# A macaron block's attention stage: normalisation of the next batch in four steps, earlier statistics, and two token tiles

## The reference, cut to what matters

```python
x = x + 0.5 * _L0_ffn_ref(_layernorm(x), ...)
x = x + _L0_attn_ref(_layernorm(x), wq, w_down, wk_up, wv_up, wo)
x = x + 0.5 * _L0_ffn_ref(_layernorm(x), ...)

def _L0_attn_ref(x, wq, w_down, wk_up, wv_up, wo):   # 16 heads of 16
    q = rope(x @ wq); lat = x @ w_down
    k = rope(lat @ wk_up); v = lat @ wv_up
    scores = einsum('bqhd,bkhd->bhqk', q, k) * scale     # 512 x 512 per head
    scores = where(page of key <= page of query, scores, min)
    return einsum('bhqk,bkhd->bqhd', softmax(scores), v) @ wo
```

## Time and profile before

| what | value |
| --- | --- |
| median of 3 runs | 1954.05 us |
| the profiled execution | 1956.1 us, span of its trace 1954.0 us |
| mean granted TensorE clock | 0.974 of full |
| PE / DVE / ACT / POOL busy | 92% / 68% / 56% / 43% |
| first and last step of attention with `x` | load issued 564.6 us, last load issued 1241.3 us |

### The profile page before, as it was taken

One profiled execution on the slowest core, in us unless ns is written; L12 is line 12 of the kernel. 1 busy time (PEld: TensorE's weight loads), 2 busy tenths in 40 slices (PEclk: granted clock), 3 DMA queues, 4 the chain that ended last, 5 costly groups with the idle time before them and its releaser, 6 DMA issues. The chain is left out here.

```text
span 1954.0 us, 31890 instructions
## 1 busy us (share of the span) xinstructions
PE 1788.5 (92%) x10553; PEld 1098.4 (56%) x10554; DVE 1337.6 (68%) x3338; ACT 1095.2 (56%) x2260; POOL 836.5 (43%) x923
## 2 busy tenths in 40 slices
PE   6999998999955789999999999999799999989998
PEld 3666665777732344444455454445455656567776
DVE  4878787566537567777777777778268787866664
ACT  4767675111114567777777777776566767631111
POOL 1111110677646565555555555551000101027777
PEclk9999999999978899999999999999999999999999
DMA  2324341899943233333333333332213243339997
GB/s 81 120 86 135 96 125 63 247 258 252 246 74 86 78 85 104 99 95 105 100 98 99 104 102 95 107 91 68 66 49 106 93 139 93 106 97 265 262 265 157
DMA packets 192653, 244.05 MB, mean 125 GB/s; under 512 B 17578, under 2 KB 159978, under 8 KB 192494
## 3 DMA queue, kind: packets, MB, share of 16 engines
q1 hardware_dynamic: 166654, 202.97, 34.6%
q0 software_dynamic: 24576, 37.77, 10.1%
q10 hardware_dynamic: 1264, 1.31, 0.2%
HBM read 126.63 MB, written 63.86 MB: 97 GB/s over the span
## 5 line engine op out<-in xcount | busy, mean ns | idle before, releaser
L1352 DVE TENSOR_REDUCE a_smax<-a_p_ring 128x1 f32<-128x512 f32 (+2 forms) x768 | 353.7, 505 | 151.7 <-PE a_p_ring L1439 146.9
L1257 ACT ACTIVATE a_probs<-a_p_ring 128x512 f32<-128x512 f32 x640 | 364.1, 607 | 103.3 <-PE a_p_ring L1451 102.1
L1439 PE MATMUL a_p_ring<-p_ks,p_qs 100*128 100x512 bf16 (+3 forms) x1024 | 244.9, 304 | 43.2 <-ACT a_probs L1257 20.0
L48 POOL TENSOR_TENSOR f_rstd<-f_mv,eps 128x4 f32<-128x4 f32 x32 | 26.2, 818 | 539.0 <-DVE f_mv L42 534.5
L1451 PE MATMUL a_p_ring<-p_qs,p_ks 103*128 103x512 bf16 (+3 forms) x1024 | 243.7, 305 | 6.0 <-ACT a_probs L1257 5.3
L648 ACT ACTIVATE e_silu<-e_p_up 128x176 f32<-128x176 f32 x128 | 40.6, 317 | 352.8 <-PE e_p_up L738 352.8
L487 PE MATMUL f_p_up<-f_xnT,ws1T 128*128 128x512 f32 x384 | 186.8, 609 | 1.1 <-ACT f_xnT L280 1.1
L528 PE MATMUL f_p_z<-ws2T,f_hidden 128*128 128x256 f32 (+1 forms) x768 | 183.9, 390 | 1.9 <-DVE f_hidden L374 1.9
L127 POOL DMA_INDIRECT h_got<-rows,slot_token x128 | 126.0, 984 | 135.1 <-DVE slot_token L464 86.1
L1467 PE MATMUL a_p_out<-a_probs,p_v 128*32 128x512 f32 (+3 forms) x2048 | 176.6, 445 | 6.5 <-ACT a_probs L1257 6.5
L487 PE MATMUL f_p_up<-f_xnT,ws3T 128*128 128x512 f32 x384 | 180.6, 593 | 0.0
(11 more groups left out here) (156 smaller groups left out, 3573.7 us busy)
## 6 DMA issues: line engine op xcount, KB each, us to landing
h_w<-w_in SPq DMA_DIRECT2D x128, 352.0 KB
p_qs<-a_parts SPq DMA_DIRECT2D x192, 128.0 KB, 2.4
p_ks<-a_parts SPq DMA_DIRECT2D x192, 128.0 KB, 2.5
h_w<-w_in SPq DMA_DIRECT2D x128, 176.0 KB
rows<-f_row SPq DMA_DIRECT2D x32, 640.0 KB, 6.4
x<-x_in SPq DMA_DIRECT2D x16, 512.0 KB, 5.9
acc<-x SPq DMA_DIRECT2D x16, 512.0 KB, 3.3
a_x<-acc SPq DMA_DIRECT2D x16, 512.0 KB, 4.0
```

Source lines behind the costliest of these rows:

```text
L1257: nc.scalar.activation(to[:], p_score[s][:], ACT.Exp, scale=SCALE).then_inc(score_free[s], 1)
L1352: ins = nc.vector.tensor_reduce(smax[:, t, 4 * g + h:4 * g + h + 1], p_score[s][:, at:at + length], AX.X, ALU.max)
L1439: ins = nc.tensor.matmul(p_score[s][:, at:at + length], qs[1 - u][0:SR + MASK, 4 * g + h, t * P:(t + 1) * P], ks[1 - u][0:SR + MASK, 4 * g ...
```

## The change

`x` becomes two tiles, batch n in `x[n % 2]`, with a load semaphore each. Batches 0 and 1 are both loaded at the start, ahead of the residual; after `XT 1` of batch j SP now loads j + 2 where it loaded j + 1. `NORM` becomes four steps of one activation each. In the turns, `STATS` move from 0.57 to 0.785 down to 0.30 to 0.43, and the one `NORM` at 0.87 becomes four at 0.595 to 0.715. In the opening lists, the statistics and normalisation of batch 1 come right after the transposes of batch 0; `V` of batch 0 and `XT` and `LAT` of batch 1 come before the first scores instead of among them; the statistics and normalisation of batch 2 move from the last tenth of `FIRST_SCORES` to 0.12 to 0.32.

```diff
-NEXT_INPUT = [(0.57, ("STATS", 0)), (0.61, ("STATS", 1)), (0.65, ("STATS", 2)), (0.785, ("STATS", 3)),
-              (0.87, ("NORM",))]
+NEXT_INPUT = [(0.30, ("STATS", 0)), (0.34, ("STATS", 1)), (0.38, ("STATS", 2)), (0.43, ("STATS", 3)),
+              (0.595, ("NORM", 0)), (0.635, ("NORM", 1)), (0.665, ("NORM", 2)), (0.715, ("NORM", 3))]
...
-FIRST_INPUT = of_batch(-2, [("XT", 0), ("XT", 1), ("Q", 0), ("LAT", 0), ("SWAP", 0), ("K", 0), ("SWAP", 1),
-                            ("Q", 1), ("K", 1), ("SWAP", 2), ("HIGH", 0), ("HIGH", 1), ("SPLIT", 0), ("SPLIT", 1),
-                            ("STACK", 0), ("SWAP", 3), ("STATS", 0), ("STATS", 1), ("STATS", 2), ("STATS", 3),
-                            ("NORM",)])
+FIRST_INPUT = (of_batch(-2, [("XT", 0), ("XT", 1), ("STATS", 0), ("STATS", 1), ("STATS", 2), ("STATS", 3),
+                             ("NORM", 0), ("NORM", 1), ("NORM", 2), ("NORM", 3),
+                             ("Q", 0), ("LAT", 0), ("SWAP", 0), ("K", 0), ("SWAP", 1), ("Q", 1), ("K", 1), ("SWAP", 2),
+                             ("HIGH", 0), ("HIGH", 1), ("SPLIT", 0), ("SPLIT", 1), ("STACK", 0)])
+               + of_batch(-1, [("V", 0), ("V", 1), ("XT", 0), ("XT", 1)]) + of_batch(-2, [("SWAP", 3)])
+               + of_batch(-1, [("LAT", 0)]))
 FIRST_SCORES = steps_of(
...
-    + at_places(-1, [(0.01, ("V", 0)), (0.03, ("V", 1)), (0.05, ("XT", 0)), (0.08, ("XT", 1)), (0.11, ("LAT", 0)),
-                     (0.15, ("Q", 0)), (0.365, ("NEG", 0)), (0.37, ("SWAP", 0)), (0.20, ("K", 0)), (0.38, ("SWAP", 1)),
+    + at_places(-1, [(0.15, ("Q", 0)), (0.365, ("NEG", 0)), (0.37, ("SWAP", 0)), (0.20, ("K", 0)), (0.38, ("SWAP", 1)),
...
-                     (0.84, ("SPLIT", 2)), (0.88, ("SPLIT", 3)), (0.89, ("STACK", 1)), (0.90, ("STATS", 0)),
-                     (0.91, ("STATS", 1)), (0.92, ("STATS", 2)), (0.93, ("STATS", 3)), (0.95, ("NORM",))]))
+                     (0.84, ("SPLIT", 2)), (0.88, ("SPLIT", 3)), (0.89, ("STACK", 1)), (0.12, ("STATS", 0)),
+                     (0.14, ("STATS", 1)), (0.16, ("STATS", 2)), (0.18, ("STATS", 3)), (0.27, ("NORM", 0)),
+                     (0.28, ("NORM", 1)), (0.30, ("NORM", 2)), (0.32, ("NORM", 3))]))
...
-        x = sb("x", [P, NT, D])
+        x = [sb(f"x{n}", [P, NT, D]) for n in range(2)]
...
-                    sp.dma_start(x[:], src[n]).then_inc(x_loaded, 16)
+                    sp.dma_start(x[n % 2][:], src[n]).then_inc(x_loaded[n % 2], 16)
 
                 load_x(0)
+                load_x(1)
...
-                        if step == ("XT", 1) and j + 1 < B:
+                        if step == ("XT", 1) and j + 2 < B:
                             sp.wait_ge(misc_free[m], used + 1)
-                            load_x(j + 1)
+                            load_x(j + 2)
...
-                def normalise(n):
-                    act.wait_ge(scales_ready, n + 1)
-                    token_normalise(nc, x, rstd, shift, x).then_inc(xn_ready, 1)
+                def normalise(n, t):
+                    if t == 0:
+                        act.wait_ge(scales_ready, n + 1)
+                    ins = token_normalise(nc, x[n % 2], rstd, shift, x[n % 2], [t])
+                    if t == NT - 1:
+                        ins.then_inc(xn_ready, 1)
```

More of the change, by code:

```diff
@@ L53, in token_scales, with token_normalise @@
     return nc.gpsimd.tensor_tensor(shift[:], shift[:], rstd[:], ALU.mult)
-def token_normalise(nc, x, rstd, shift, xn):
-    for t in range(NT):
+def token_normalise(nc, x, rstd, shift, xn, tiles=range(NT)):
+    for t in tiles:
         last = nc.scalar.activation(xn[:, t, 0:D], x[:, t, :], ACT.Identity, bias=shift[:, t:t + 1],
@@ L1064, in attention @@
         pairs_ready = sem("pairs_ready")
-        x_loaded = sem("x_loaded")
+        x_loaded = [sem(f"x_loaded{n}") for n in range(2)]
         residual_loaded = sem("residual_loaded")
@@ L1307, in turn @@
                         elif kind == "NORM":
-                            normalise(j + 1)
-                normalise(0)
+                            normalise(j + 1, step[1])
+                for t in range(NT):
+                    normalise(0, t)
                 turns(act, turn)
@@ L1318, in statistics @@
                     if t == 0:
-                        dve.wait_ge(x_loaded, 16 * n + 16)
+                        dve.wait_ge(x_loaded[n % 2], 16 * (n // 2) + 16)
                         wait_count(dve, scales_ready, n)
-                    nc.vector.bn_stats(stats[:, t, :], x[:, t, :])
+                    nc.vector.bn_stats(stats[:, t, :], x[n % 2][:, t, :])
                     if t == NT - 1:
@@ L1512, in turn @@
                                 ins = nc.tensor.transpose(p_misc[m][:, t * P:(t + 1) * P],
-                                                          x[:, t, step[1] * P:(step[1] + 1) * P], w.ident[:])
+                                                          x[j % 2][:, t, step[1] * P:(step[1] + 1) * P], w.ident[:])
                             ins.then_inc(misc_ready[m], 1)
```

## The result

Four runs of the changed kernel gave a median of 1926.73 us (1923.00 to 1931.83), four of the kernel before 1954.17 us (1953.21 to 1956.65): ratio 0.9852, 95% interval 0.9832 to 0.9872. The forecast was 1927, the range 1919 to 1940. A second series gave 1931.94 against 1955.87, ratio 0.9865 (0.9841 to 0.9888).

What follows compares the result with a forecast made beforehand. PE was taken as the limit, losing time only in waits. Opening -4.4 and -7.8, turn 0 +0.8, twelve turns -15.5: -26.9 us from 1956.1 gives 1929.2; the median lies 2.05 lower, so 1927 us, range 1919 to 1940.

Steps and rivals of the forecast that it cites:

- The turns: Twelve full attention turns: -1.53 us from moving `NORM`, +0.24 from early statistics, so -1.29 each and -15.5 in all.
- The 1.53 us from start to start at the old place: PE's delay at a score bank behind `NORM`'s old place, 938.94 to 940.47 in turn b = 5; claimed to go entirely.
- The cost of the early statistics: Full turns: `STATS` moved earlier on DVE delay the reduction that frees `WO.1`'s bank, costing PE 0.24 us.
- the bank of group B's last exponential: Full turns: `S1.2.C.0` wants this bank 0.3 us earlier, costing PE some 0.2 us, swallowed by the 0.57 us wait behind.
- `PV.2.B`'s exponential: Full turns: group B's last exponential, delayed by `NORM` pieces, ends at 929.8, just before `PV.2.B` at 929.98; margin 0.2 us.
- POOL's gap: Full turns: `scales` needs 1.9 us of POOL's 2.54 idle before 922.00; done at 921.8, margin 0.3 us for the statistics.
- POOL's full stretch: Turn 0: POOL has no idle time, so `scales` ahead of the chain to the maxima's parts costs +1.9 us.
- the wait behind `NORM`: Turn 0: PE's wait of 1.14 us at 699.24 goes.
- The opening: Before turn 0: first scores -4.4 us through earlier `NEG.0`; its end -7.8 us through a removed wait and low clock.
- the low clock: Opening's end: PE at 1.2 GHz behind the 4.98 us wait, from 654.56; its removal was taken as -2.8 us.
- the second rival: Full turns gain nothing because another chain already ends with PE; only opening and turn 0 gain, -11.4, 1943 us; 7%.
- a fall behind waits of 2.5 us in each turn: Rival of `scales` missing POOL's gap: PE's clock drops behind each wait, about 2 us more per turn; 1974 us, 7%.

Runs made afterwards that it cites:

- the run with the block at the old place: Changed kernel with the early `STATS` kept but `NORM` as four back-to-back steps at 0.87; attention 817.7 us, turn 47.85 us.
- the run with `scales` behind `SWAP.2`: Changed kernel with `STATS 3` moved from 0.43 to 0.455; attention 829.4 us, turn 48.74 us, one run of 1949.47 us.
- late statistics: `STATS` at 0.57 to 0.785, `NORM` at 0.87 to 0.96: in all turns of the changed kernel (814.7 us attention), or in turn 0 alone (802.2).
- the last version: Changed kernel with `NORM` at 0.53, 0.535, 0.54, 0.925, `SPLIT 2` at 0.752, and turn 0's statistics late; median 1918.13 us, ratio to before 0.9811.
- the run that it was made from: Changed kernel with `NORM` at 0.53, 0.535, 0.54, 0.925 and `SPLIT 2` at 0.752 behind `MAX 0`; attention 804.8 us, turn 46.80 us.

## Why the prediction was right

The two gains that it rests on, `NORM`'s place in the turns and the opening, came by the steps that it names. Its sum was -26.9 us and attention became 28.0 us shorter; that the median then came within 0.3 us of 1927 is luck, since what stands behind attention alone took 538.9 to 546.2 us in the traces of the runs.

**The turns.** -1.29 us each was worked out, -1.38 measured. The 1.53 us from start to start at the old place came to the hundredth. The cost of the early statistics was put at 0.24 us at `WO.1`; it is 0.11 there, and 0.20 in POOL's chain to the copy of the maxima, in after as in the run with the block at the old place. The wait for that copy was to stay at 0.6 us and is 0.35, because PE loses some 0.5 us in two small stalls ahead of it; the bank of group B's last exponential costs its foretold 0.2 us as a stall that the waits' list leaves out (the start at 917.03 is 0.44 behind the one before, in place of 0.22). The rows:

```profile
916.59 0.38 PE L1458 MATMUL a_p_ring<-p_qs,p_ks 103*128 103x256 bf16 x2
917.03 0.39 PE L1446 MATMUL a_p_ring<-p_ks,p_qs 100*128 100x256 bf16 x2
917.35 1.07 PE L1474 MATMUL a_p_out<-a_probs,p_v 128*32 128x384 f32 x16
```

**The margins.** `PV.2.B`'s exponential and POOL's gap were said to fit by 0.2 and 0.3 us. Neither shows a wait, but both were nearer than these numbers say. The exponential ends 34.07 us behind `XT 0` (916.36 plus 0.61, less 882.90), 0.26 later than the 929.8 less 895.99 of the prediction, more than its margin; `PV.2.B` itself starts 0.46 us later in the turn than before, and the wait for the maxima's copy takes that back. `scales` ends 25.95 us behind `XT 0`, and `SWAP.2` started at 26.01 before, so 0.06 us was left in the old gap; 0.26 are seen because `SWAP.2` has become 0.20 later. That POOL's gap decides was shown by the run with `scales` behind `SWAP.2`.

**Turn 0.** +0.8 us was worked out, +1.9 for POOL's full stretch and -1.1 for the wait behind `NORM`. Measured from the second `V` of turn 0 to that of turn 1 it is 42.09 us before (661.23 to 703.32) and 42.71 after (652.98 to 695.69), +0.6. `MAX 0` divides it (690.46 and 684.04): up to there 29.23 us before and 31.06 after, +1.8, and from there 12.86 and 11.65, -1.2, so both terms came. Only the waits look otherwise: the one for the maxima's parts was forecast as 5.5 us and is 3.1, since the exponential ahead of it is waited for as well, for 1.9. First the row of before, then those of after:

```profile
703.32 1.04 PE L1535 MATMUL a_p_ring<-p_wv,a_latT 128*128 128x256 f32 x4
```

```profile
652.98 1.03 PE L1542 MATMUL a_p_ring<-p_wv,a_latT 128*128 128x256 f32 x4
...
680.55 0.39 PE L1458 MATMUL a_p_ring<-p_qs,p_ks 103*128 103x384 bf16 x2 [1.90 <-ACT a_probs L1263]
684.04 0.59 PE L1512 MATMUL a_p_ring<-p_ident,p_smax_parts 128*128 128x128 bf16 x4 [3.10 <-POOL p_smax_parts L1201]
...
695.69 1.04 PE L1542 MATMUL a_p_ring<-p_wv,a_latT 128*128 128x256 f32 x4
```

That the order of `scales` and maxima is what costs there was shown: late statistics gave 41.8 us in two runs, and in the last version `MAX 0` comes 1.86 us earlier behind `XT 0` than in the run that it was made from.

**The opening.** -12.2 us was worked out. Counted from the first `XT`, the second `V` of turn 0 stands at 86.98 us before and 74.98 after: -12.0. `NEG.0`, in POOL's rows, and the first `S1` in PE's:

```profile
617.87 0.31 POOL L1193 TENSOR_SCALAR a_smax_rest<-a_smax 128x32 f32<-128x32 f32 x1 [4.44 <-DVE a_smax L1354]
```

```profile
598.30 3.75 PE L1528 MATMUL a_p_ring<-a_xnT,p_w_down 128*128 128x512 f32 x4 [4.47 <-ACT a_xnT L1273]
602.09 2.38 PE L1446 MATMUL a_p_ring<-p_ks,p_qs 100*128 100x512 bf16 x12
...
649.70 0.39 PE L1458 MATMUL a_p_ring<-p_qs,p_ks 103*128 103x512 bf16 x1
```

Less the 3.75 us by which this attention began later, `NEG.0` is at 614.1 (614.0 was forecast, 618.44 before) and the first `S1` at 598.3, as before. The second is in part luck: `LAT` of batch 1, put at 1.9 us, ran at the lower clock behind a wait of 4.47 us (granted 0.50 from 598 to 602 us) and took 3.75, up to the moment at which the first `S1` starts; any longer, and it would have held that back. One statement was wrong in place, not in size: turn 0 was to start at 643 us, and starts at 649.70 less 3.75, 646.0. I had taken the 2.8 us of the low clock off before the turn's start, but they are gained within its first 6 us: from turn 0's first score bank to its second `V` were 5.66 us before (655.57 to 661.23) and are 3.28 now (649.70 to 652.98), so 2.4 us and not 2.8.

**PE as the limit.** Weight loads are busy 52 of 100 us, and still PE had no slack in the turns: its waits that were taken away or added came out in the turn's length (47.10 us in after, 47.85, 47.54, 48.74 and 46.80 in the variants), and with that the second rival fell. The page that the prediction weighed (Trainium skill, "Trainium Kernel Development and Optimization", Performance Expectations) calls matmul busy time a bad metric for how close a kernel is to roofline, that is to the most the hardware could do; it does not say which engine sets the length of a turn. The prediction left that condition out and read PE's slack from it; that step does not hold.

## What to carry to other kernels

When several engines follow one hand-written order, put a step that another engine feeds into the idle time of both: look at the feeder's gap (here 2.54 us on POOL for 1.9 us of work) before the user's, since missing it cost 1.64 us a turn, where all the new places together had gained 1.38. Cut a block of short instructions in front of others' work into single ones where the engine behind has only a slack of a few banks, and then ask at each later wait, not only at the one removed, whether the lateness is used up. When an edit moves stalls without shortening the turn, look for the parallel chain and remove both; and measure inside the trace, from one landmark to another, when the stages around vary by more than the effect.

## What was not expected of the hardware

PE's clock fell without a long wait just ahead. In the opening after, `S2` and `S1` banks of 0.38 us each begin to take 0.61 us at 626.88. The waits ahead of it are 0.77 us at 621.83 and then 0.2 to 0.4 us each, one in front of nearly every bank; PE is busy 1.5 of the 2.5 us from 624.0 to 626.5, still at a granted clock of 1.00, and from 628 to 632 us the granted clock is 0.50:

```profile
625.17 0.38 PE L1458 MATMUL a_p_ring<-p_qs,p_ks 103*128 103x512 bf16 x1 [0.36 <-DVE a_smax L1359]
...
626.28 0.39 PE L1458 MATMUL a_p_ring<-p_qs,p_ks 103*128 103x512 bf16 x1 [0.21 <-DVE a_smax L1354]
626.88 0.61 PE L1458 MATMUL a_p_ring<-p_qs,p_ks 103*128 103x512 bf16 x1 [0.21 <-DVE a_smax L1359]
```

It is nothing of the change: before, the banks slow down at 626.52 in the same way. The Trainium skill ("TensorE: Matmul & The Clock Gate", HAM oscillation) tells of clock loss through idle gaps between bursts of matmuls; no such gap stands here, PE did single banks at DVE's pace. No run was made to test the cause. In the full turns the granted clock stayed at 1.00, also with five waits a turn of up to 0.67 us (`scales` behind `SWAP.2`). The prediction had weighed a fall behind waits of 2.5 us in each turn; whether one would come could not be seen, since the waits stayed shorter.
